# Second layer of a four-layer graph network: one ring of row tiles for input and residual, bias added by VectorE; first layer reordered

## What is computed

```
h = relu(layernorm(x)); x1 = h @ W1 + b1             # 1024 -> 512
g = x1; four times: g += gated, normed sum of g over the edges
x += concat(x1, g)                                   # first layer
h = relu(layernorm(x)); x += h @ Wt + bias           # second: Wt is built from
                                                     # edge_weight, 1024 x 1024
h = relu(layernorm(x)); x += relu(A (h @ W2) + b2)   # third: A is 1250 x 1250
h = relu(layernorm(x)); x += elu(attention(h @ W3))  # fourth
```

## Time and profile before

| | us |
|---|---|
| median of three runs | 944.64 (944.01 to 945.78) |
| the profiled execution's own time | 954.86 |
| its span, first to last instruction | 953.1 |
| PE busy in the span | 929.8 |
| granted TensorE clock, mean | 0.993 |

### The profile page before, as it was taken

The page is one execution under the profiler, slowest core; times in us unless marked ns, Lnnn a source line. Parts: engine busy times, 40 slices in busy tenths (PEclk is TensorE's granted clock), DMA queues, the critical chain, the costliest instruction groups (busy, mean ns, idle before and its releaser), DMA issues.

```text
span 953.1 us, 13269 instructions
## 1 busy us (share of the span) xinstructions
PE 929.8 (98%) x4815; PEld 768.4 (81%) x4816; DVE 727.5 (76%) x1261; ACT 476.1 (50%) x732; POOL 142.8 (15%) x229
## 2 busy tenths in 40 slices
PE   5999999999999999979999899999999999999998
PEld 3888788888888888868888788888888888888887
DVE  7999889888987988358744483698858875977786
ACT  5677764544644656124334344544633224666654
POOL 3111200000000010323331000014310000323331
PEclk9999999999999999998999899999999999999999
DMA  7242920040050043799965210043987524211222
GB/s 263 90 134 89 103 72 1 1 110 0 0 154 22 0 96 93 147 297 272 286 200 210 88 42 30 0 56 102 230 199 222 171 93 83 89 45 54 79 88 84
DMA packets 48505, 104.70 MB, mean 110 GB/s; under 512 B 6296, under 2 KB 23388, under 8 KB 48304
## 3 DMA queue, kind: packets, MB, share of 16 engines
q1 hardware_dynamic: 38080, 76.69, 24.7%
q0 software_dynamic: 10368, 27.27, 14.8%
HBM read 62.51 MB, written 46.67 MB: 115 GB/s over the span
## 4 chain that ended last, share of the span: by engine, by line
PE 87%; DMA 5%; DVE 4%; issue 1%; ACT 1%; POOL 1%; SPq 0%; DVEq 0%; ACTq 0%; POOLq 0%
PE ps L774 20%; PE ps L2636 13%; PE ps L2611 10%; PE ps L2516 9%; PE ps L2518 9%; PE ps L2517 9%; PE ps L2580 4%; PE ps L2584 3%; PE ps L2435 2%; PE ps L2436 2%; PE ps L2437 2%; DMA count_squares<-count_squares 1%; PE ps L757 1%; DMA squares_of_rows<-squares 1%; DMA xin<-x_after 1%
## 5 line engine op out<-in xcount | busy, mean ns | idle before, releaser
L2516 PE MATMUL ps<-g_hi,mask_hi 128*128 128x512 f32 x400 | 157.8, 394 | 0.4 <-DVE mask_lo L1859 0.4
L2518 PE MATMUL ps<-g_hi,mask_lo 128*128 128x512 f32 x400 | 155.9, 390 | 0.0
L2517 PE MATMUL ps<-g_lo,mask_hi 128*128 128x512 f32 x400 | 155.8, 390 | 0.0
L1317 ACT ACTIVATE mask<-ps,v 128x640 f32<-128x640 f32 x80 | 63.1, 793 | 86.1 <-PE ps L2518 47.0
L2636 PE MATMUL ps<-y_all,att_hi 128*128 128x512 f32 x380 | 103.6, 392 | 0.0
L2516 PEld LDWEIGHTS ps<-g_hi,mask_hi 128*128 128x128 f32 x400 | 75.1, 188 | 19.7 <-DVE mask_lo L1859 2.3
L2518 PEld LDWEIGHTS ps<-g_hi,mask_lo 128*128 128x128 f32 x400 | 75.1, 188 | 16.0
L2517 PEld LDWEIGHTS ps<-g_lo,mask_hi 128*128 128x128 f32 x400 | 75.2, 188 | 14.8
L2611 PE MATMUL ps<-w_hi,parts 128*128 128x512 f32 x280 | 86.7, 389 | 0.0
L774 PE MATMUL ps<-w,hT_hi 128*128 128x512 f32 x320 | 85.7, 390 | 0.0
L2636 PEld LDWEIGHTS ps<-y_all,att_hi 128*128 128x128 f32 x380 | 70.4, 188 | 14.8 <-issue 0.4
(11 more groups left out here) (252 smaller groups left out, 1930.4 us busy)
## 6 DMA issues: line engine op xcount, KB each, us to landing
xin<-x_after SPq DMA_DIRECT2D x20, 512.0 KB, 5.5
squares_of_rows<-squares SPq DMA_DIRECT2D x15, 512.0 KB, 4.7
turned<-squares_of_rows SPq DMA_DIRECT2D x60, 128.0 KB, 3.1
x_after<-g POOLq DMA_DIRECT2D x20, 256.0 KB, 7.0
x_after<-row_all POOLq DMA_DIRECT2D x10, 512.0 KB, 8.1
xres<-x_after POOLq DMA_DIRECT2D x10, 512.0 KB, 5.7
x_after<-xres POOLq DMA_DIRECT2D x10, 512.0 KB, 4.8
xin<-in_x SPq DMA_DIRECT2D x9, 512.0 KB, 3.9
```

What stands on the lines that cost most here:

```text
L1317: nc.scalar.activation(mask[k][:, :], U_ALL, ACT.Tanh, bias=v[:, s:s + 1]).then_inc(tanh_ready, 1)
L2516: nc.tensor.matmul(SUMS[dd], mask_hi[k][:, cols], g_hi[:, s, :], start=(s == 0), stop=False)
L2517: nc.tensor.matmul(SUMS[dd], mask_hi[k][:, cols], g_lo[:, s, :], start=False, stop=False)
L2518: last = nc.tensor.matmul(SUMS[dd], mask_lo[k][:, cols], g_hi[:, s, :], start=False, stop=(s == T - 1))
```

## The change

Second layer: the rows are loaded once, into a ring of four tiles that takes the place of `xin` and `xres`. `h_act` writes its result to tiles of its own (`h_rows`); DVE adds the bias (`bias_of`) and then the product in the ring's tile. The ten accumulating transfers and the ten loads by POOL are gone. SP's order becomes: store squares of t, load the turned tile t, load rows of t+1. The load of tile t waits until tile t-4 is stored and read. In the third layer TURNED_IN changes. In the first layer PE transposes tile 1 and picks the parts in the midst of tile 0's product, opens the second bank ahead of that product's last block, and runs nineteen matmuls of zeros (ZERO_PRODUCTS) between its first steps; ACT's order follows.

```diff
-TURNED_IN = ((0, 1, 2), (3, 4, 5), (6, 7), (8,), (9,), ())
+TURNED_IN = ((0,), (1, 2, 3), (4, 5, 6), (7,), (8,), (9,))
+ZERO_PRODUCTS = (9, 4, 6)
...
+    ring = [xres[0], xres[1], xin[0], xin[1]]
+    h_rows = {t: at(f"h_rows{t}", [P, D], F32, R_Y + (60 if t == 1 else 68 if t % 2 == 1 else 76) * KIB) for t in range(T)}
...
     def h_act(act, d, i, b):
-        act.wait_ge(shift_ready, d.tiles(2 * i + b + 1))
-        nc.scalar.activation(xin[b][:, :], xin[b][:, :], ACT.Relu, bias=shift[:, b:b + 1]).then_inc(h_ready, 1)
+        t = 2 * i + b
+        act.wait_ge(shift_ready, d.tiles(t + 1))
+        if d.n == 1 and t == 3:
+            act.wait_ge(mask_used, 2 * GATES * T)
+        elif d.n == 1 and t >= 2 and t - 2 < FIRST_SQUARED[1]:
+            act.wait_ge(h_transposed[b], d.turns(t // 2, b))
+        elif d.n == 1 and t >= 2:
+            act.wait_ge(squares_ready, d.squared(t - 2))
+        nc.scalar.activation(h_of(d, t)[:, :], x_of(d, t)[:, :], ACT.Relu, bias=shift[:, b:b + 1]).then_inc(h_ready, 1)
...
         def load_x1(t):
             sp.wait_ge(half_stored[t // 2], 32)
-            sp.dma_start(xin[t % 2][:, :], x1_dram[rows(t), :]).then_inc(xin_landed[t % 2], 16)
+            if t == 0:
+                sp.wait_ge(w_lo_ready, KT * 2)
+            elif t in (2, 3):
+                sp.wait_ge(xin_landed[t % 2], 16 * d.norm_pairs(t // 2))
+            elif t >= 4:
+                sp.wait_ge(hs_h_ready, t - 3)
+                sp.wait_ge(stored[t % 2], 16 * (t // 2 - 1))
+            sp.dma_start(ring[t % 4][:, :], x1_dram[rows(t), :]).then_inc(xin_landed[t % 2], 16)
...
         for t in range(FIRST_SQUARED[1], T):
             store_squares(sp, d, t)
-            if t + 2 < T:
-                load_x1(t + 2)
             load_turned(sp, d, t)
+            if t + 1 < T:
+                load_x1(t + 1)
...
-        pool.wait_ge(bias_landed, 32)
-        add_bias(0)
-        add_bias(1)
-        pool.wait_ge(w_lo_ready, KT * 2)
-        load1(0)
-        add_bias(2)
-        load1(1)
         for t in range(T):
             pool.wait_ge(product_read[t % 2], d.pairs(t // 2 + 1))
-            pool.dma_start(x2_dram[t * P:(t + 1) * P, :], xres[t % 2][:, :]).then_inc(stored[t % 2], 16)
+            if t >= 2:
+                pool.wait_ge(stored[t % 2], 16 * (t // 2))
+            pool.dma_start(x2_dram[t * P:(t + 1) * P, :], ring[t % 4][:, :]).then_inc(stored[t % 2], 16)
             if t % 2 == 1 and t + 1 < T:
                 scale_pair_pool(pool, d, (t + 1) // 2)
-            if t + 3 < T:
-                add_bias(t + 3)
             if t % 2 == 1:
                 hs_scale_pool(pool, t // 2)
-            pool.wait_ge(stored[t % 2], 16 * (t // 2 + 1))
-            if t + 2 < T:
-                load1(t + 2)
...
             if n < COUNT_RING:
-                act.wait_ge(squares_ready, d.squared(T - 1))
+                for b in range(2):
+                    act.wait_ge(stored[b], 16 * (HT - 1))
+                act.wait_ge(hs_h_ready, T - 2)
...
+        def bias_of(t):
+            if t == 0:
+                dve.wait_ge(bias_landed, 32)
+            dve.wait_ge(h_ready, d1.tiles(t + 1))
+            nc.vector.tensor_tensor(ring[t % 4][:, :], ring[t % 4][:, :], row_all[:, :], ALU.add).then_inc(bias_in, 1)
...
         variance1(1)
+        bias_of(0)
         for t in range(1, T - 1):
...
             if t == 2:
                 self_loops()
+            bias_of(t)
             if t + 3 < T:
                 stats_dve(dve, d1, (t + 3) // 2, (t + 3) % 2)
...
         def x1_pe(t):
-            if t == 1:
-                pe.wait_ge(blend_chain, 3)
-                open_bank(1)
-            if t + 1 < T and t + 1 != LATE_TILE:
+            if 0 < t < T - 1 and t + 1 != LATE_TILE:
                 transpose_pe(pe, d0, (t + 1) // 2, (t + 1) % 2)
             for k in range(KT):
+                if t == 0 and k == 2:
+                    transpose_pe(pe, d0, 0, 1)
+                if t == 0 and k == 3:
+                    pick_parts()
+                if t == 0 and k == KT - 1:
+                    pe.wait_ge(blend_chain, 3)
+                    open_bank(1)
...
         open_bank(0)
+        zero_products(ZERO_PRODUCTS[0], PRODUCT0[1])
         transpose_pe(pe, d0, 0, 0)
         sum_rows_below()
+        zero_products(ZERO_PRODUCTS[1], PRODUCT0[1])
         pick_edges()
```

More of the change, by code:

```diff
@@ L427, in build_program @@
     degrees_ready = sem("degrees_ready")
-    bias_placed_in = sems("bias_placed_in", 2)
+    bias_in = sem("bias_in")
     weights_stored = sems("weights_stored", 2)
@@ L605, in split_wt_dve, with x_of, h_of @@
                                     ALU.subtract).then_inc(w_lo_ready, 1)
+    def x_of(d, t):
+        return ring[t % 4] if d.n == 1 else xin[t % 2]
+    def h_of(d, t):
+        return h_rows[t] if d.n == 1 else xin[t % 2]
     def stats_dve(dve, d, i, b):
@@ L611, in stats_dve @@
         for half in range(2):
-            nc.vector.bn_stats(stats[b][:, half, :], xin[b][:, half * 512:(half + 1) * 512]).then_inc(ln_chain, 1)
+            nc.vector.bn_stats(stats[b][:, half, :], x_of(d, t)[:, half * 512:(half + 1) * 512]).then_inc(ln_chain, 1)
         settled(dve, ln_chain, LN_STEPS * d.tiles(t) + 2)
@@ L756, in transpose_pe @@
         for k in range(KT):
-            last = nc.tensor.transpose(TRANSPOSED[:, k * P:(k + 1) * P], xin[b][:, k * P:(k + 1) * P], ident[:, :])
+            last = nc.tensor.transpose(TRANSPOSED[:, k * P:(k + 1) * P], h_of(d, t)[:, k * P:(k + 1) * P], ident[:, :])
         last.then_inc(h_transposed[b], 1)
@@ L896, in load_x1 @@
             sp.wait_ge(half_stored[t // 2], 32)
-            sp.dma_start(xin[t % 2][:, :], x1_dram[rows(t), :]).then_inc(xin_landed[t % 2], 16)
-        for t in range(2):
-            sp.wait_ge(h_transposed[t], d.turns(0, t))
-            load_x1(t)
+            if t == 0:
[7 more added lines that the diff above has]
+        for b in range(2):
+            sp.wait_ge(h_transposed[b], d.turns(0, b))
+        load_x1(0)
+        load_x1(1)
         sp.dma_start(row_all[:, :], bias1.partition_broadcast(P)).then_inc(bias_landed, 16)
-        for t in range(2, FIRST_SQUARED[1] + 2):
-            sp.wait_ge(h_transposed[t % 2], d.turns(t // 2, t % 2))
-            load_x1(t)
+        load_x1(2)
+        load_x1(3)
         for t in range(FIRST_SQUARED[1], T):
             store_squares(sp, d, t)
-            if t + 2 < T:
-                load_x1(t + 2)
             load_turned(sp, d, t)
-        for b in range(2):
-            sp.wait_ge(bias_placed_in[b], 16 * HT)
+            if t + 1 < T:
+                load_x1(t + 1)
+        sp.wait_ge(bias_in, T)
         sp.dma_start(row_all[:, :], b2.partition_broadcast(P)).then_inc(bias_landed, 16)
@@ L1198, in _ @@
         for k in range(KT):
-            if k == 2:
+            if k == 1:
                 place_bias(0)
@@ L1206, in _, with take_parts @@
             nc.scalar.activation(edges[0:EP, n, :], PICKED[n][0:EP, 1, :], ACT.Copy).then_inc(picked_copied, 1)
-        act.wait_ge(parts_picked, 3)
-        for n in range(2, 5):
-            nc.scalar.activation(edges[0:EP, n, :], PICKED[n][0:EP, 1, :], ACT.Copy).then_inc(picked_copied, 1)
+        def take_parts():
+            act.wait_ge(parts_picked, 3)
+            for n in range(2, 5):
+                nc.scalar.activation(edges[0:EP, n, :], PICKED[n][0:EP, 1, :], ACT.Copy).then_inc(picked_copied, 1)
         def number_sources():
@@ L1253, in _ @@
             if t == 0:
+                place_bias(1)
                 number_sources()
+                take_parts()
                 widen_rows()
@@ L1257, in _ @@
                 widen_cells()
-            if t + 1 < T and t % 2 == 0:
+            if 0 < t < T - 1 and t % 2 == 0:
                 place_bias(t + 1)
@@ L1389, in hs_relu @@
                 act.wait_ge(hT_lo_ready, dense[1].tiles(t + 1))
-            nc.scalar.activation(hs_f[:, :, t, 1, :], xres[t % 2][:, :].rearrange("p (h n) -> p h n", n=HID), ACT.Relu,
+            nc.scalar.activation(hs_f[:, :, t, 1, :], ring[t % 4][:, :].rearrange("p (h n) -> p h n", n=HID), ACT.Relu,
                                  bias=hs_minus[:, t % 2:t % 2 + 1]).then_inc(hs_h_ready, 1)
@@ L1971, in hs_stats_of @@
             for half in range(2):
-                hs_step_done(nc.vector.bn_stats(stats[b][:, half, :], xres[b][:, half * 512:(half + 1) * 512]))
+                hs_step_done(nc.vector.bn_stats(stats[b][:, half, :], ring[t % 4][:, half * 512:(half + 1) * 512]))
             dve.wait_ge(hs_chain, hs_steps[0])
@@ L2028, in _ @@
         hs_lo_of(T - 3)
+        bias_of(T - 1)
         residual(T - 1)
@@ L2350, in pick_edges, with pick_parts @@
                 pick(PICKED[n], lambda t: of[0:EDGE_ROWS, t, :]).then_inc(ends_picked, 1)
+                zero_products(ZERO_PRODUCTS[2] * n, SPENT)
+        def pick_parts():
             pe.wait_ge(parts_chain, 5)
@@ L2408, in open_bank, with zero_products @@
```

(3 more changed lines are left out.)

16 lines of the change are left out of this document (4 added, 12 removed).

## The result

| | before | after |
|---|---|---|
| median, us | 945.21 (944.01 to 950.65, 4 runs) | 958.00 (957.47 to 959.51, 4 runs) |
| the profiled execution's own time | 954.86 | 958.49 |
| its span | 953.1 | 956.7 |
| granted TensorE clock, mean | 0.993 | 0.996 |

The changed kernel is slower: 1.0111 times the time before, 95% interval 1.0081 to 1.0141. Forecast were 941.3 us and a range of 937 to 951, so the time lies outside the range, on the side of rival B. The two profiled executions differ by 3.6 us only, the medians by 12.8. That difference is part of the story: the profile that the prediction rested on shows an execution of the kernel before that was slower than most of its runs.

A forecast was written before the change was run, and what follows sets the result against it. PE was taken to bound the kernel before, and from the second layer's tile 4 on a ring of waits. First layer -2.0, second layer +4.3, count passes -5.6 give -3.3 us; from 944.6 that is 941.3 us, range 937 to 951.

The forecast's parts named there:

- rival B: Second layer's ring slower, store 4.0 and load 4.3 us: layer 12.8 us longer, kernel 949.8 us; chance 0.27.
- Taking the difference over to the median: Last step: the -3.3 us summed on the profiled execution, applied to the runs' median of 944.6 us, gives 941.3 us.
- 8.1 us ahead of tile 3: Second layer's product: PE's 5.3 us wait for a low part plus 2.8 us of slow clock, expected to go.
- Second layer's product: Stall goes, but a ring of waits through all queues paces the tiles; stage ends at 511.5 us, 4.3 us longer.
- the load beside the turned loads: Second layer's ring: landing time of the row load beside the tail of the turned loads, taken as 3.7 us.
- the sign of being wrong: Prediction wrong as a whole if load or store in the second layer's ring differs by 0.7 us from that taken.
- the even period: Second layer's ring: time from square to square in an even step, put at 12.8 us.
- the quickest of each row: Second layer with store 2.65, 2.9 and load 3.1 us: periods of 12.1 and 13.2 us, stage ends at 508.
- Count passes: One count tile instead of three before the first bank reading; PE's wait and the clock's fall go, 5.6 us gained.
- First layer: Tile 0's product starts earlier with other steps inside it: 2.0 us gained, bounds 0 and 3.9.
- the zeros cost nothing: First layer: nineteen matmuls of zeros stand where PE waits for other engines; otherwise six cost at most 2.8 us.
- The entry of the second layer: Tile 0's load waits for the last weight split; bounds 0 and 1.1 us lost, taken as 0.

The follow-up runs named there:

- again: The kernel before, unchanged, profiled a second time: 946.82 us, ratio 1.0002.
- deep: The changed kernel with six tiles in the ring and the load of rows two tiles ahead, in front of the turned loads: 939.95 us, 0.9904 of the kernel before.
- deep_again: The six-tile ring kernel with the load two ahead and in front of the turned loads, run again unchanged: 940.47 us, 0.9898 of the kernel before.
- first_only: The kernel before with only the first layer's new order and its nineteen matmuls of zeros: 944.48 us, 0.9978 of the kernel before.
- deep_late: The changed kernel with six ring tiles instead of four, the load still behind the turned loads: 954.84 us, 1.0070 of the kernel before.
- ahead: The changed kernel with SP issuing the load of rows ahead of the four turned loads, ring still four tiles: 952.08 us, 1.0020 of the kernel before.
- both: The kernel before with the new first layer and the new TURNED_IN, its second layer untouched: 943.35 us, 0.9949 of the kernel before.
- second_only: The changed kernel with the old first layer and the old TURNED_IN: 965.67 us, 1.0203 of the kernel before.
- deep_old_turned: The six-tile ring kernel (load two ahead, in front of the turned loads) with the old TURNED_IN: 945.45 us, 0.9952 of the kernel before.
- no_bias: The kernel before without the second layer's ten accumulating transfers, so its bias is missing from the output: 945.64 us, 0.9970 of the kernel before.
- deep_no_zeros: The six-tile ring kernel (load two ahead, in front of the turned loads) without the nineteen matmuls of zeros: 941.50 us, 0.9920 of the kernel before.

## Why the prediction was wrong

The forecast missed by 958.0 - 941.3 = 16.7 us. It splits into four parts: 9.7 us of the last step, 3.9 of the product, 1.7 of the count passes and 1.3 of the first layer (the sum is 0.1 short by rounding).

**Taking the difference over to the median: 9.7 us. This is the step that failed.** The prediction knew that the profiled execution of before "itself lies 10.2 us above the median of the runs" and took that as an offset common to both kernels. After the change it is 0.5 us (958.49 against 958.00). Most of the 10 us were the very stalls that I then counted as gains, 8.1 us ahead of tile 3 and 5.6 in the count passes: of the 8.2 us between the spans of the two profiles of the kernel before, 6.2 lie in the product and 1.8 on the way to the fourth layer. `again`, an execution near the median, has 2.0 us of gap without low clock and 2.2 with one stretch of 3.4 us. Against that profile the difference in span is 956.7 - 944.9 = 11.8 us: -0.5 for the start, +14.5 for the product (127.0 - 112.5), -2.3 up to the fourth layer, +0.1 behind it. That is the 12.8 us of the medians within the spread. Rival B had the right mechanism and sign and was given 0.27. Its 4.3 us for the load was right, its 4.0 for the store of the squares was not (2.6), and its 949.8 us rests on the same offset.

**Second layer's product: predicted +4.3, in the two first profiles +8.2 (127.0 - 118.8).** The mechanism was right: DVE waits for the load in every step, the squares are 13.3 to 14.6 us apart, and PE has gaps of 0.8 to 3.7 us ahead of tiles 3 to 8. Tile 4's square came at 417.1 (predicted 418.2), the load's issue 6.0 to 6.2 us after the square (6.0), the statistics led to the square in 3.0 and 4.15 us (3.0 and 4.15), and product 8 began 5.35 us behind square 9 (5.3). Mis-sized was one term, the load beside the turned loads: 4.0 to 5.0 us against my 3.7. Five periods took 70.1 us instead of 66.2, and 3.6 of these 3.9 us are the load's (4.4 us on average, 0.7 above my 3.7, which the prediction itself named as the sign of being wrong). The row of 4.3 us from the fourth layer was the nearer one. Two of the prediction's sums don't come out of its terms: the even period is 12.7 and not 12.8 us, and the quickest of each row gives periods of 11.8 and 13.0 and an end near 506, not 12.1, 13.2 and 508; its 2.65 us for a store stands in none of its rows (the ring's stores took 2.6). Neither changes what it says. The Trainium skill, "DMA: Bandwidth & Descriptors", section "Anatomy of one DMA — SWDGE (gpsimd) path", whose figures gave an estimate of 3.2 us for 512 KB, agrees with the store by POOL (3.2 us in the median). SP's transfers of the same size, to which the prediction also put the 3.2 us, took 2.6 (squares) and 4.0 to 5.0 us (rows).

**Count passes: predicted -5.6, in the two first profiles -3.9 (188.4 - 192.5 is -4.1, of which 0.1 comes back behind).** Right as a mechanism: no wait for a bank and the clock at 1.00. What is missing is the stall of 1.1 us at the end of pass 0, for which the profile shows no cause. It comes and goes: `deep` has 186.8 us here, without any wait, and the same kernel in deep_again 188.4, with two such stalls of 0.9 and 0.4 us. Against 186.8 the first profile of before is 5.7 us longer, the 5.6 of the prediction. Worth of the order in time: 2.3 us in the kernel before, 5.0 in `deep`.

**First layer: predicted -2.0, seen -0.7.** Tile 2's transposes do come 3.0 us earlier (22.77 against 25.82), as predicted; the product begins only 0.7 us earlier. In time, first_only gained 2.1 us (0.9978, interval 1 to 3), so the 2.0 may have been right as a number; the way that the prediction gives for it, the new order, is not what the profiles show. I said that the zeros cost nothing, and no profile shows a cost; I missed that they are what pays.

The entry of the second layer, priced at 0, has no wait of PE for a mask's low part from 340 us on in the changed profile, as predicted.

## What to carry to other kernels

When a profiled execution is 1% slower than the timed ones, find its excess before pricing anything: a stall that only part of the executions have is not a gain of its full size in the median, and a second profile of the same kernel tells, as does the granted clock of each timed run. When a change takes away transfers but makes the next load wait for the end of this step's work, go once round the circle and add up every issue, landing and instruction; if the sum exceeds the bound engine's time per tile, the bandwidth saved is worth nothing. Of two branches of nearly the same length, opening one alone gains only a part: here 3 us (deep_late) and 6 us (ahead), the 6 mostly because the load itself got quicker. A ring of six tiles with the load two ahead and in front of the turned loads opened both, 18 us, and turned a loss of 1.1% into a gain of 1.0%, of which the two other parts, in `both`, bring half.

## What the runs showed of the hardware

- A load of 512 KB that was issued right behind four transfers of 128 KB landed after 4.0 to 5.0 us (the changed kernel; 4.4 to 5.0 in deep_late), ahead of them after 3.4 to 3.7 (`ahead`); the four then took 4.0 instead of 3.2 us in the median. Being ahead of them is not all: in `deep` the load also stands ahead of the four, but 0.5 us behind a store of 512 KB, and took 4.3 to 4.4 us.
- The clock does not fall behind every gap. In the changed kernel, starts of matmuls lay 3.4 us apart at 433.3 us with no fall, 3.5 us apart at 447.4 with a fall at 452.2, and 3.7 us apart at 475.6 with a fall at 479.5, each of 3.4 us. Behind each gap in the product or the count passes of the fourteen profiles that brought a fall, 3.4 or 6.8 us ran at 1.2 GHz, and the length of the gap does not tell which: 6.8 us followed starts 2.8 us apart (first profile of before, 534.0 us), 3.6 (second_only), 4.3 (deep_late), 4.5 (deep_old_turned) and 5.6 (first profile of before); 3.4 us followed starts from 2.0 (first_only) up to 4.5 us apart (second_only).
- Nineteen matmuls of zeros at 2 to 13 us had the clock at 2.4 GHz by 13.5 us, 1.4 us at the end of the gated sums. The row of the granted clock does not show the difference: it reads 1.00 at 10 to 20 us in deep_no_zeros too, where matmuls start 0.43 us apart. At a program's start, go by the matmuls' pace.
- Times of one kernel can spread by 1%. The kernel before: 9.6 us over 25 runs on one chip and 2.9 us over 22 on another. Without the ten accumulating transfers, on the first of these chips: 3.3 us over 12 runs (no_bias), 2.0 over 4 (deep_again), 2.3 over 6 (deep_no_zeros), but 4.8 over 10 where the old TURNED_IN left its stall (deep_old_turned).
